# Attention core with its maxima as a row of the contraction, two buffers of queries and keys, scores three steps behind the looks

## The chip, the cores and the metric

One core of a Trainium2 chip runs the whole program. The metric is device microseconds of one execution. TensorE does matrix products, VectorE and ScalarE work on its results, GpSimd helps and issues transfers, SyncE only issues transfers (DMAs).

## The reference

Input x is 4 images of 16x16 positions with 192 channels, float32. Four blocks follow each other; each adds a mixer and a feed-forward part to x, each behind a layer norm. The mixers of blocks 0, 2 and 3 are attentions with 12 heads of 16 channels over the 256 positions of an image. This is blocks 2 and 3:

```python
attn = einsum('bqc,bkc->bqk', q * SCALE, k)
attn = attn + rel_h[..., :, None] + rel_w[..., None, :]   # rel_h, rel_w: q times tables of relative position
attn = softmax(attn, axis=-1)
out = einsum('bqk,bkc->bqc', attn, v)
```

Block 0 is a local attention: every position sees 9 neighbours at distance 1, 2 or 3 (by head), positions outside the image count as zeros. Block 1's mixer is a Fourier mixer, and the feed-forward parts are mixtures of experts; the change leaves their arithmetic alone.

## The kernel before

`attention(net, m, prep)` is called for l0, l2 and l3 (attention 0, 2, 3). First TensorE projects x to queries, relative terms, keys and values (`project_tensor`, `project_scalar`, `project_vector`). Queries and keys are split into a high and a low part, so that one product with reduced precision over stacked parts gives the full one; `store` writes the parts to `q_scratch` and `k_scratch` in DRAM, and `load_queries` and `load_keys` bring them back with 128 stacked rows in the one pair of buffers `q_parts`, `k_parts`. The load of a new image's piece (4, 2, 4, 2 heads) waits until the scores of the same heads of the image before are done. One-hot rows in the keys (from `onehot_scratch`) and, in l0, rows of 0 or a huge negative number in the queries (`near_scratch`) add the positional terms and the mask.

The core goes by pairs of heads: 6 pairs an image, 4 images, 24 steps (n). All engines run the same list of steps, each its own part, in an order written out by hand; the first image (on GpSimd the first two) is unrolled, the rest is a loop over images:

- `look` (TensorE, L803): queries times keys, positions of the query on the partitions, two banks of PSUM for the two heads.
- `maximum` (VectorE, L917): one reduction over the pair gives the negated row maxima; in l0 L921 lets the padding in.
- `shift` (L990 GpSimd, L926 VectorE): identity times maxima, a diagonal matrix per head and half.
- `score` (TensorE, L815 and L816): keys times queries, transposed against the look, and on top a product of ones with the shift, which subtracts each query's maximum. It comes 2 steps after the look in l0, 1 step after in l2 and l3.
- `exponential` (ScalarE, L877) writes the probabilities; `mix_quad` (TensorE, L854) multiplies them with v for four heads; `take_mix` (ScalarE, L883) copies, `turn` (TensorE, L823) transposes back, `finish` (VectorE, L942 to L954) divides by the row sum.

In the core SyncE loads the next images (`load_image`) and stores a part of the images 2 and 3, GpSimd stores the rest of them piece by piece between shifts (`store_rest`), stages v (`stage_v`, L981) and in l0 stores the finished heads. Tables for later blocks (`prep.third`) go out from SyncE in groups of four in l0. `attention_output` then projects the result; in l0 it first rereads it from DRAM (L1041).

## Time and profile before

| | us |
|---|---|
| median of 3 runs | 777.36 |
| runs | 773.33 to 778.35 |
| the profiled execution (its span) | 779.2 |
| first look to last finish, attention 0 | 37.4 to 109.4 |
| attention 2 | 391.1 to 455.7 |

The profiled execution's own time beside its span is not listed separately; the span, from the first to the last instruction, is used for it. Times of rows count from the start of the span. Engines in the rows: PE is TensorE's matmul, PEld its weight load, DVE is VectorE, ACT ScalarE, POOL GpSimd, SP SyncE; a name with q is the engine's queue. A group's "idle before" is time in which the engine did nothing, and the arrow names what ended it. The granted clock of TensorE is a share of full speed (2.4 GHz); 0.50 is the lower of its two levels.

### The profile page before, as it was taken

To read this page: it belongs to the slowest core of one execution; us is meant where nothing else is said; L and a number is where in the kernel's file an instruction comes from. 1 tells how busy PE (TensorE), PEld (TensorE's weight loads), DVE (VectorE), ACT (ScalarE), POOL (GpSimd) and SP (SyncE) were. 2 spreads that over 40 slices of the span, in tenths; PEclk is the share of its full clock that TensorE was granted. 3 is DMA by queue.
4 is the path that set the end of the run, shared out by engine and by line. 5 is a ranking of instruction groups with operands and counts; after the bars stand their busy time and mean duration, and the time that the engine had idled before them with its cause. 6 is when DMAs were issued, how large, how long until landed. Compare 5 with 4: busy or idle time off the path is not lost. (4 is left out here: it accounts for less than half of the span.)

```text
span 779.2 us, 14121 instructions
## 1 busy us (share of the span) xinstructions
PE 707.0 (91%) x4658; PEld 612.0 (79%) x4658; DVE 392.7 (50%) x983; ACT 301.7 (39%) x604; POOL 227.0 (29%) x271
## 2 busy tenths in 40 slices
PE   4987988999998999998888988899999896999997
PEld 2566767897796899995676778699999666777996
DVE  4466746015345443335678756334435476875301
ACT  3334533332413344424444552233452253555323
POOL 4166620002100044442055301723344204531000
PEclk9989999899999999999979999989999998999999
DMA  3735540534106166533788403567772279850352
GB/s 92 197 107 150 143 115 22 142 102 121 30 1 179 45 167 167 127 48 71 207 203 217 102 17 117 156 156 167 185 174 28 55 188 236 227 121 1 101 135 70
DMA packets 94011, 95.22 MB, mean 122 GB/s; under 512 B 18881, under 2 KB 80213, under 8 KB 93945
## 3 DMA queue, kind: packets, MB, share of 16 engines
q1 hardware_dynamic: 80568, 75.11, 36.6%
q0 software_dynamic: 11712, 18.18, 11.4%
q10 hardware_dynamic: 1680, 1.28, 0.6%
q8 instruction: 29, 0.48, 0.3%
q14 instruction: 22, 0.17, 0.1%
HBM read 66.92 MB, written 27.84 MB: 122 GB/s over the span
## 5 line engine op out<-in xcount | busy, mean ns | idle before, releaser
L2130 POOL DMA_INDIRECT sum_scratch<-area,f_row_index x48 | 72.4, 1509 | 172.3 <-DVE area L2053 157.0
L917 DVE TENSOR_REDUCE neg_max<-psum 128x4 f32<-128x1024 f32 x72 | 88.0, 1222 | 32.9 <-PE psum L803 32.0
L1804 PE MATMUL psum<-w,area 128*112 128x192 f32 (+1 forms) x576 | 96.2, 326 | 0.0
L1804 PEld LDWEIGHTS psum<-w,area 128*112 128x112 f32 (+1 forms) x576 | 93.5, 183 | 0.0
L990 POOL TENSOR_TENSOR shift<-ident,neg_max 128x256 fp32r<-128x256 f32 x96 | 66.5, 704 | 89.1 <-DVE neg_max L917 57.4
L295 PE MATMUL psum<-ident 128*128 128x128 f32 x624 | 82.0, 289 | 5.1 <-issue 1.9
L295 PEld LDWEIGHTS psum<-ident 128*128 128x128 f32 x624 | 77.9, 204 | 7.2 <-issue 5.9
L815 PE MATMUL psum<-q_parts,k_parts 128*128 128x256 f32 x288 | 79.6, 306 | 0.3
L803 PE MATMUL psum<-k_parts,q_parts 128*128 128x256 f32 x288 | 56.0, 321 | 25.9 <-DMA k_parts<-k_scratch 15.0
L816 PE MATMUL psum<-shift,ones_r 128*128 128x256 f32 x288 | 75.2, 292 | 0.0
L803 PEld LDWEIGHTS psum<-k_parts,q_parts 128*128 128x128 f32 x288 | 42.7, 208 | 38.6 <-issue 20.7
L1911 DVE TENSOR_TENSOR q_parts<-w,q_parts 128x1536 fp32r<-128x1536 f32 x16 | 28.1, 1756 | 81.4 <-ACT q_parts L1841 81.4
L815 PEld LDWEIGHTS psum<-q_parts,k_parts 128*128 128x128 f32 x288 | 57.9, 201 | 10.4 <-issue 8.2
L877 ACT ACTIVATE area<-psum 128x512 f32<-128x512 f32 x96 | 52.4, 595 | 30.2 <-PE psum L816 30.1
L816 PEld LDWEIGHTS psum<-shift,ones_r 128*128 128x128 f32 x288 | 57.9, 201 | 0.0
L587 PE MATMUL psum<-x_wide,l_w 96*96 96x512 f32 x96 | 44.7, 622 | 3.5 <-PEq L158 2.8
L1869 ACT ACTIVATE area<-psum,b 128x384 f32<-128x384 f32 x48 | 27.9, 582 | 49.5 <-PE psum L1790 46.6
L1387 PE MATMUL psum<-x_wide,w 96*128 96x256 f32 x192 | 42.8, 381 | 1.0 <-DMA b<-in_f_b_dram 0.9
L1468 DVE TENSOR_TENSOR mixed<-psum,b 128x384 f32<-128x384 f32 x8 | 4.5, 558 | 77.7 <-PE psum L1399 77.7
L1387 PEld LDWEIGHTS psum<-x_wide,w 96*128 96x128 f32 x192 | 36.0, 190 | 6.6 <-DMA b<-in_f_b_dram 1.7
L854 PE MATMUL psum<-area,v_stage 128*32 128x256 f32 x384 | 39.4, 386 | 0.0
L587 PEld LDWEIGHTS psum<-x_wide,l_w 96*96 96x96 f32 x96 | 16.1, 171 | 28.9 <-issue 28.9
(258 smaller groups left out, 1329.9 us busy)
## 6 DMA issues: line engine op xcount, KB each, us to landing
w<-in_f_w_dram SPq DMA_DIRECT2D x32, 576.0 KB, 5.0
w<-in_f_w_dram SPq DMA_DIRECT2D x16, 384.0 KB, 4.7
w<-in_f_w_dram SPq DMA_DIRECT2D x32, 192.0 KB, 5.0
q_parts<-q_scratch SPq DMA_DIRECT2D x32, 192.0 KB, 3.5
q_scratch<-area SPq DMA_DIRECT2D x22, 192.0 KB, 2.2
k_parts<-k_scratch SPq DMA_DIRECT2D x63, 64.0 KB, 3.1
q_parts<-q_scratch SPq DMA_DIRECT2D x32, 96.0 KB, 2.9
q_parts<-q_scratch SPq DMA_DIRECT2D x40, 64.0 KB, 3.2
```

The source lines that it names most:

```text
L295: pe.matmul(net.psum[:, bank, 0:P], net.ident[:, :], net.ident[:, :], start=True, stop=True)
L587: ins = pe.matmul(ps[0:HC, bank, :], m.w[:, k, D * j + HC * half:D * j + HC * (half + 1)], net.x_chan[:, k, 512 * tc:512 * (tc + 1)], star ...
L803: ins = pe.matmul(ps[:, b, IMG_TOK * c:IMG_TOK * (c + 1)], query(2 * s + b, c), k_parts[:, 2 * s + b, :], start=True, stop=True)
L815: pe.matmul(out, k_parts[:, h, keys], query(h), start=True, stop=False)
L816: ins = pe.matmul(out, net.ones_r[:, :], net.shift[:, s % 2, b, :, :], start=False, stop=True)
L854: ins = pe.matmul(ps[32 * (h % 4):32 * (h % 4 + 1), 6, 0:IMG_TOK], net.v_stage[:, k, h, :], net.probs_t[h // 2 % 3][:, h % 2, k, :], start ...
L877: act.activation(net.probs_t[s % 3][:, b, :, :].rearrange("p k t -> p (k t)"), ps[:, 2 + 2 * (s % 2) + b, :], ACT.Exp).then_inc(exp_done, 1)
L917: ins = dve.tensor_reduce(most, ps[:, 0:2, :].rearrange("p b (c k) -> p (b c) k", c=2), AX_X, ALU.max, negate=True)
L990: ins = nc.gpsimd.tensor_tensor(*shift_of(n, s, b))
L1387: ins = pe.matmul(ps[:, 3 * b + fc // 2, IMG_TOK * (fc % 2):IMG_TOK * (fc % 2 + 1)], net.w1[0:HC, b, k, P * fc:P * (fc + 1)], net.x_chan[: ...
L1804: ins = pe.matmul(out, x.hidden[:, fc, R * c:R * (c + 1)], net.w2[:, b, fc, :], start=(fc == 0), stop=(fc == FCH - 1))
L2130: pool.indirect_dma_start(net.sum_dram[:, :], bass.IndirectOffsetOnAxis(ap=row_index[0:size, b, c:c + 1], axis=0), x.y[0:size, b, c, :], N ...
```

## The change

What it does:

- The negated maximum of each query becomes one more row of the contraction in the score (row `MAX_ROW` of `q_parts`, ones in the same row of `k_parts`). `maximum` now works head by head; `turn_maximum` (TensorE) transposes the pair's maxima [128, 4] to [4, 128] in PSUM, `take_row` (ScalarE) copies them to `max_rows`, and `set_row` (SyncE) writes them into the row with a DMA of 2 KB. Shifts and their matmuls go, with them `ones` and the memsets of `q_parts` at the start.
- `q_parts` and `k_parts` have a second buffer each (`Second`); images alternate. Loads go by halves of 6 heads. Image 0's come from SyncE and GpSimd, all others from GpSimd (`load_half`). The constant rows are loaded for both buffers in l0 and l2, for one in l3.
- `store_rest` stores the images 2 and 3 together, in 4 (l0) or 10 (l2, l3) DMAs, all from GpSimd behind the loads of image 1, and GpSimd waits for their landing before the loads of image 2 and before v of image 1 is staged.
- Looks are by head and alternate with the scores of three steps before (`BEHIND = 3`). The order of a step on TensorE: look head 0 of pair n, score head 0 of n-3, turn of the maxima of n-1, look head 1, score head 1, then the mix of a quad in odd steps and its turn in even ones. All steps are unrolled.
- The tables of the Fourier mixer are loaded in `attention_output` of l0, before the reread; the other tables go out one behind each `set_row`. `experts` takes a tile of its own (`marks`) in place of `shift`.

```diff
+BEHIND = 3
...
+    MAX_ROW = K0 + HD if m.local else K0 + QROWS
...
+            def set_row(n):
+                i, s = divmod(n, PAIRS_OF_HEADS)
+                sp.wait_ge(max_row_sb, n + 1)
+                dst = q_parts[i % 2][MAX_ROW:MAX_ROW + 1, 2 * s:2 * s + 2, :].bitcast(F32)
+                sp.dma_start(dst.rearrange("p n (c t) -> p (n c) t", c=2), net.max_rows[:, s % 3, :].bitcast(F32)).then_inc(row_set[s % 3], DMA)
...
+            for n in range(ALL_PAIRS):
+                set_row(n)
+                if prep:
+                    start_loads(net, sp, itertools.islice(tables, 1), prep.loaded)
...
-            def look(i, s):
-                need(pe, max_ready, n)
-                for b in range(2):
-                    for c in range(2):
-                        ins = pe.matmul(ps[:, b, IMG_TOK * c:IMG_TOK * (c + 1)], query(2 * s + b, c),
+            def look(n, b):
+                need(pe, max_ready, 2 * n + b - 1)
+                for c in range(2):
+                    ins = pe.matmul(ps[:, b, IMG_TOK * c:IMG_TOK * (c + 1)], q_parts[buf][0:MAX_ROW, h, P * c:P * (c + 1)],
+                                    k_parts[buf][0:MAX_ROW, h, :], start=True, stop=True)
...
+            def turn_maximum(n):
+                if m.local:
+                    pe.wait_ge(max_known, n + 1)
+                else:
+                    pe.wait_ge(max_ready, 2 * n + 2)
+                need(pe, max_row_sb, n)
+                pe.transpose(ps[0:4, 7, 0:P],
+                             net.neg_max[:, 2 * s:2 * s + 2, :].rearrange("p n c -> p (n c)"), net.ident[:, :]).then_inc(max_turned, 1)
...
-                        pe.matmul(out, k_parts[:, h, keys], query(h), start=True, stop=False)
-                        ins = pe.matmul(out, net.ones_r[:, :], net.shift[:, s % 2, b, :, :], start=False, stop=True)
+            def score(n, b):
+                need(pe, exp_done, 2 * (n - 2) + b + 1)
+                if b == 0:
+                    pe.wait_ge(row_set[s % 3], DMA * (2 * i + s // 3 + 1))
+                for k in range(2):
+                    ins = pe.matmul(ps[:, 2 + 2 * (s % 2) + b, IMG_TOK * k:IMG_TOK * (k + 1)],
+                                    k_parts[buf][0:MAX_ROW + 1, h, P * k:P * (k + 1)], q_parts[buf][0:MAX_ROW + 1, h, :],
+                                    start=True, stop=True)
...
+            for n in steps:
+                if is_pair(n - BEHIND):
+                    exponential(n - BEHIND, 0)
+                if is_pair(n - 1):
+                    take_row(n - 1)
+                if is_pair(n - BEHIND):
+                    exponential(n - BEHIND, 1)
+                if quad_of(n, 2) is not None:
+                    take_mix(quad_of(n, 2))
...
+            def load_half(i, half):
+                need(pool, scored, (i - 2) * HEADS + HALF_HEADS * (half + 1))
+                load_queries(pool, i, half, loaded[i % 2][half])
+                load_keys(pool, i, half, loaded[i % 2][half])
...
+            pool.wait_ge(first_loaded[0], per_load)
+            for half in range(2):
+                load_half(1, half)
...
+            store_rest(pool)
+            pool.wait_ge(rest_written, DMA * rest_count)
+            for i in range(IMGS - 1):
+                if i + 2 < IMGS:
+                    load_half(i + 2, 0)
+                stage_v(i + 1, 0)
...
+            fourier_loads = fourier.loads(dram)
+            prep.third += fourier_loads
+            attention_output(net, l0, norm, [(gate.loads, gate.loaded), (fourier_loads, prep.loaded)], gate.mean)
```

## Rows read from the trace of the kernel before

**Rows 1.** By line, maxima: attention 0, 2, 3, stretches of 0, 2 (ns min/median/max)

```profile
L917 DVE TENSOR_REDUCE neg_max<-psum x24: 1208/1225/1226, 39.4 to 100.5; 128x4 f32<-128x1024 f32 x24
L917 DVE TENSOR_REDUCE neg_max<-psum x24: 1211/1224/1225, 392.3 to 449.1; 128x4 f32<-128x1024 f32 x24
L917 DVE TENSOR_REDUCE neg_max<-psum x24: 1212/1224/1226, 650.0 to 705.1; 128x4 f32<-128x1024 f32 x24
L917 DVE TENSOR_REDUCE neg_max<-psum x6: 1225/1225/1225, 88.4 to 100.5; 128x4 f32<-128x1024 f32 x6
L917 DVE TENSOR_REDUCE neg_max<-psum x7: 1215/1225/1225, 435.0 to 449.1; 128x4 f32<-128x1024 f32 x7
```

**Rows 2.** Attention 2, busy by stretch (counts), granted clock, DMA share, GB/s

```profile
391.00:398.70 7.70, 6.32 (x28) 6.06 (x28) 5.31 (x8) 1.95 (x4) 3.58 (x6) 0.50 0.92 214
398.70:455.70 57.00, 52.45 (x478) 41.58 (x477) 42.93 (x79) 29.14 (x58) 27.05 (x44) 1.00 0.57 144
```

**Rows 3.** Timeline, attention 0: start, length, engine, line, operation

```profile
49.95 1.09 PE L854 MATMUL psum<-area,v_stage 128*32 128x256 f32 x16
...
77.15 0.38 PE L823 MATMUL psum<-ident,mix_chan 128*128 128x128 f32 x2
77.67 0.74 PE L803 MATMUL psum<-k_parts,q_parts 128*128 128x256 f32 x4
78.45 1.22 DVE L917 TENSOR_REDUCE neg_max<-psum 128x4 f32<-128x1024 f32 x1 [0.43 <-PE psum L803]
79.09 0.28 PE L816 MATMUL psum<-shift,ones_r 128*128 128x256 f32 x1
79.88 0.17 DVE L942 TENSOR_TENSOR pad_exp<-pad_exp,pad_count 128x8 f32<-128x8 f32 x1
80.55 0.37 ACT L883 COPY mix_chan<-psum 128x256 f32<-128x256 f32 x1 [0.16 <-PE psum L854]
80.62 0.36 DVE L954 TENSOR_TENSOR mixed<-psum,inv_sum 128x64 f32 x2
```

**Rows 4.** Timeline of attention 0, the look that begins image 2

```profile
71.50 1.22 PE L803 MATMUL psum<-k_parts,q_parts 128*128 128x256 f32 x4 [3.81 <-DMA k_parts<-k_scratch]
```

**Rows 5.** Costliest groups of the page: the exponentials

```profile
L877 ACT ACTIVATE area<-psum 128x512 f32<-128x512 f32 x96 | 52.4, 595 | 30.2 <-PE psum L816 30.1
```

**Rows 6.** DMA: attention 2 in sum; median us to landing, quiet, full queues

```profile
DMA packets 10136, 9.83 MB, mean 154 GB/s; under 512 B 1867, under 2 KB 9492, under 8 KB 10132
...
f_slot_number<-in_f_slot_number_dram SPq DMA_DIRECT2D x1, 1.5 KB, 1.8
...
k_parts<-k_scratch ACTq DMA_DIRECT2D x3, 32.0 KB, 5.0
```

**Rows 7.** Looks grouped, attention 0, 2, 3; timeline of ends of 0, 2

```profile
L803 PE MATMUL psum<-k_parts,q_parts x96: 278/283/575, 37.4 to 100.2; 128*128 128x256 f32 x96
L803 PE MATMUL psum<-k_parts,q_parts x96: 274/283/582, 391.1 to 448.8; 128*128 128x256 f32 x96
L803 PE MATMUL psum<-k_parts,q_parts x96: 278/283/582, 648.8 to 704.8; 128*128 128x256 f32 x96
...
109.02 0.36 DVE L954 TENSOR_TENSOR mixed<-psum,inv_sum 128x64 f32<-128x64 f32 x2
...
451.16 0.39 PE L815 MATMUL psum<-q_parts,k_parts 128*128 128x256 f32 x1
455.36 0.36 DVE L954 TENSOR_TENSOR mixed<-psum,inv_sum 128x64 f32<-128x64 f32 x2
```

**Rows 8.** Timeline of the output stage of attention 0

```profile
111.24 0.39 SPq L1041 DMA_DIRECT2D mixed<-o_scratch  x1
116.54 1.04 PE L1068 MATMUL psum<-ident,mixed 128*96 128x128 f32 x8
```

**Rows 9.** Timeline of the start, and landing of the input

```profile
3.58 2.65 POOL L289 MEMSET q_parts<- 64x3072 f32 x1
...
x_res<-in_x_dram ACTq DMA_DIRECT2D x1, 384.0 KB, 4.5
```

More of the change, by code:

```diff
@@ L646, in project_scalar @@
         for b in range(4):
-            if b == 2:
-                act.wait_ge(first_written[of_keys], 2 * DMA)
-                for piece in range(2):
-                    load_keys(act, 0, piece)
             act.wait_ge(k_sb, b + 1)
@@ L758, in _ @@
+            tables = iter(prep.third if prep else ())
             for n in range(of_keys + 1):
                 store_first(n)
+            for n in range(0, of_keys, 2):
+                written(n)
+            load_queries(sp, 0, 0, first_loaded[0])
+            store_first(of_keys + 1)
             for half in range(2):
-                for n in range(half, of_keys, 2):
-                    written(n)
-                for piece in (2 * half, 2 * half + 1):
-                    load_queries(sp, 0, piece)
@@ L856, in mix_quad, with turn @@
                 ins.then_inc(mixed_ps, 1)
-            project_tensor(pe)
-            for _ in all_steps(pe, step):
-                pass
-            last = IMGS * PAIRS
-            if behind == 2:
-                score(last - 2, PAIRS - 2)
-            mix_quad(IMGS - 1, GROUPS - 2)
-            score(last - 1, PAIRS - 1)
-            turn(IMGS * GROUPS - 2)
-            mix_quad(IMGS - 1, GROUPS - 1)
-            turn(IMGS * GROUPS - 1)
+            def turn(quad):
+                pe.wait_ge(mix_sb, quad + 1)
+                for c in range(2):
+                    ins = pe.transpose(ps[:, 6, IMG_TOK + P * c:IMG_TOK + P * (c + 1)], net.mix_chan[:, P * c:P * (c + 1)], net.ident[:, :])
+                ins.then_inc(turned, 1)
@@ L955, in finish @@
                 ins.then_inc(mixed_sb, 1)
[L957 to L973 removed]
+            project_vector(dve)
+            for n in steps:
+                for b in range(2 if is_pair(n) else 0):
+                    maximum(n, b)
+                if m.local and is_pair(n):
+                    allow_padding(n)
+                if quad_of(n, 3) is not None:
+                    finish(quad_of(n, 3))
         @block.gpsimd
@@ L1019, in _ @@
+            for n in range(1, of_keys, 2):
+                pool.wait_ge(first_written[n], 2 * DMA)
+            load_queries(pool, 0, 1, loaded[0][1])
             pool.wait_ge(v_sb, 1)
@@ L1520, in __init__ @@
         self.low = net.sb("tokens_low", [P, TILES, D], F32R)
[L1521 to L1522 removed]
+        self.is_slot = [spare[:, TILES * D:TILES * D + SLOTS_MAX], *(net.marks[:, n, :] for n in range(2))]
         free = rest
```

416 lines of the change are left out of this document (174 added, 242 removed).

## The prediction

> **What bounds the kernel now.** I looked first at what attention costs and what holds its step. Each of the three attentions runs 24 head pairs. Grouped by line, the row maxima start at 39.4 and end at 100.5 us in attention 0, at 392.3 to 449.1 in attention 2, at 650.0 to 705.1 in attention 3; undisturbed stretches give 12.1/5 = 2.43 us a step in attention 0 and 14.1/6 = 2.35 in attention 2 [rows 1]. By stretch, TensorE is busy 52.5 of 57 us at a granted clock of 1.00, but 0.50 in the first 7.7 us [rows 2]: a core stage starts at half clock. In the timeline of two steps at full clock [rows 3] the eight score matmuls end with one at 79.09, 1.42 us after the look began at 77.67, twelve matmuls in all, so one costs 0.12 us. A mix of a quad takes 1.09 us [rows 3]; its turn, two transposes, 0.24 at the same pace (0.38 busy with the drain). Two steps are thus 24 x 0.12 + 1.1 + 0.24 = 4.2 us of TensorE against 4.7 measured; the rest is waiting for the maximum. So TensorE bounds attention 2 and 3 to about 90%; in attention 0 VectorE is close behind, and a load comes late once: the look at 71.50 waited 3.8 us for keys [rows 4].
>
> **The change, part by part.** All by hand from durations at full clock.
>
> *Shift matmuls out.* Per pair four of twelve matmuls go (96 per attention, 0.12 us apart) [rows 3]: -0.48 us. Added is one transpose of the maxima, no row has its shape; between 0.12 (half of a turn's 0.24) and 0.38 (its busy time with the drain) [rows 3]; I take 0.13, since the drain is not waited for by TensorE. Two steps: 16 x 0.12 + 0.26 + 1.1 + 0.24 = 3.5, with waits 3.75: 1.87 us a step.
>
> *Maximum by head.* A reduction of 1,024 elements takes 1.22 us [rows 1]. One of 512 has no row: from 0.61 (half) to 0.78 (half with a further 0.17, what the smallest VectorE operation here costs [rows 3]); I take 0.69. Four in two steps: 2.76. The finish of a quad in attention 0 runs from 79.88 to 80.98, 1.1 us [rows 3]; with the padding operations, 0.6 per two steps, and gaps that makes 4.7 us, 2.35 a step: VectorE bounds attention 0 (2.2 to 2.5), so little of the matmul saving shows there. In attention 2 and 3 the finish has no padding, 0.6 us: 3.5 in two steps, below TensorE's 3.75. The two heads' banks alternate, so the next look no longer waits for the whole pair. GpSimd's 1.2 us of shifts a pair goes, off the path.
>
> *The row's way.* Score of pair m comes three steps after its look; its maxima are turned one step after. From the end of score (m-2, head 0), all on one chain: drain 0.3, an exponential that stands ahead on ScalarE 0.6 [rows 5], the copy of the row 0.25 (between 0.17, above, and the 0.37 of a copy of 128x256 [rows 3]), semaphores and SyncE 0.1, then the DMA, L. It must fit in two steps less one score: step >= 0.75 + L/2. The smallest loads land after 1.8 us in an idle stretch; a 32 KB one took 5.0 us with the queues full [rows 6]. This row is 2 KB, on a queue that holds nothing else in attention 2 and 3: nearest to the first. I take 2.0 quiet and 2.7 while bulk runs, so 1.75 hidden under 1.87, and 2.1 exposed. In attention 0 (2.35) up to L = 3.2 is hidden. But SyncE also issues one weight table behind each row there; two of these are 432 KB, some 2 us of transfer in front of the next row: +2.
>
> The Trainium skill ("DMA: Bandwidth & Descriptors", section "Queues, rings and completion order") says that a DMA engine goes round its queues packet by packet. By that rule bulk on GpSimd's queue would delay a row hardly at all; the 5.0 us row speaks against, though that transfer stood behind three of its own queue. The rule makes a rival below.
>
> *Fill and tail.* From the first look to the first score, three steps of looks alone: half-clock look and two reductions 2.4, turn and copy 0.8, SyncE 0.1, L 2.7: 6. In attention 0 VectorE is still with the values at that time: 7. The tail: look 23 to score 23 is 4.7 (reduction 1.0, turn, copy, L); score 23 to the last finish is as before, 451.16 to 455.7 = 4.6, and 5.0 in attention 0, ending at 109.4 [rows 7].
>
> *Half clock.* TensorE is idle in the fill, so it starts the dense part at the low level; I give it 4 us there, in which one step passes instead of two.
>
> *Loads and buffers.* The second buffer lets image i+1 load during image i: the 3.8 us wait goes, with the half-clock steps behind it; 23 x (2.66 - 2.43) = 5.3 us in attention 0 [rows 1, 4]. The price: GpSimd now issues all of it in one queue, image 1 (by the code 12 DMAs of 160 rows of 12 KB, 1.97 MB in attention 2 and 3), then the stores of images 2 and 3 in one piece (10 DMAs, 3.1 MB), waits for their landing, and only then loads image 2; behind that wait stands the staging of v for image 1, for which TensorE's mix of quad 3 waits in step 11. 9.83 MB moved in 64 us at a mean share of 0.61 [rows 2, 6], so 250 GB/s at full. 0.3 + 1.97 + 3.1 = 5.4 MB are 21.5 us, and image 2's first half another 4: 26 to 29 us after the start with landings. Step 12 is due at 6 + 4 + 17 = 27: +1 in attention 2 and 3. In attention 0 only 3.3 MB stand ahead, 13 us, due at 30: none. Also, half 0 and half 1 of image 0's queries now load side by side, and the first look needs six heads in place of four: +1 at the start of attention 2 and 3, nothing in attention 0, whose queries are a third.
>
> The skill's same page (section "SWDGE vs HWDGE vs iDMA") warns that VectorE can hold up GpSimd's writing of descriptors. It would lengthen this queue; GpSimd's issues beside busy VectorE show no sign here, and it is part of the rival on bulk below.
>
> *Sums by attention.* Attention 2: 6 + 4 + 5.7 steps x 2.1 (bulk running, 12) + 13.3 x 1.9 (25.3) + 1 (later bulk) + 1 (image 2) + 4.7 + 4.6 = 58.6, after +1 at the start: 59.6 for 64.7 (391.1 to 455.7 [rows 7]): -5. Attention 3 is 63.0 now (648.8 to 705.1, and 6.6 from the last maximum to the end as in attention 2 [rows 1, 7]): +1 as well, -3.4. Attention 0: 7 + 4 + 19 x 2.35 + 4.7 + 5.0 + 2 (tables) = 67.4 for 72.0 (37.4 to 109.4): -4.6.
>
> *Beside the core.* The nine Fourier tables (1.2 MB) move from attention 0 to its output stage, on SyncE's queue ahead of the reread of image 3. That reread is issued at 111.24 and used at 116.54 [rows 8]; an issue takes 0.39 and a gap [rows 8], nine some 3.8, which puts it at 115, and 1.2 MB stand before it, 4.9 us: lands at 118.5, +2. Its bounds are 0 (projection hides all) and 4. The two memsets at the start end at 6.23, the input has landed at 0.89 + 4.5 = 5.4, and the barrier is at 6.5 [rows 9]: -0.6. Unrolling the image loop changes no count; no idle time by instruction fetch shows at the loop's ends, so 0.
>
> Sum: -5 - 3.4 - 4.6 + 2 - 0.6 = -11.6 us. The profiled execution spans 779.2, 1.8 above the median 777.36, so 777.4 - 11.6 = **766 us**.
>
> **Rivals.** *More: the steps run at TensorE's own pace* (by the round-robin rule of the skill cited above this is what follows). L stays at 2.0 under bulk, no wait for image 2, first look not later, a reduction of 0.62. Then attention 2 is 6 + 4 + 19 x 1.87 + 9.3 = 54.8 (-9.9), attention 3 -8.1, attention 0 at 2.2 a step -9.5; with -0.6: 749 to 750. For it: every term taken away is an allowance, none is in a row. Against: queues at 0.92 share early in the core [rows 2].
>
> *Slower: the row's DMA is the bound.* If L is 3.5 on average, a step is 0.75 + 1.75 = 2.5 in all three. The point is L = 3.2: there the step equals the 2.35 of now. Attention 2: 6.8 + 4 + 47.5 + 5.7 + 4.6 + 1 = 69.6 (+4.9), attention 3 +6.6, attention 0 7.8 + 4 + 47.5 + 5.7 + 5.0 + 2 = 72.0 (0), +2 and -0.6: 790. For: a wait on three other engines and a queue now lies in each step, and the 32 KB transfer landed after 5.0 us [rows 6]. Against: it is 16 times larger and had others of its own queue ahead.
>
> *No change: bulk or clock eats it.* Image 2 comes 5 us later in attention 2 and 3 (200 GB/s in place of 250 gives this), or gaps in TensorE's stream keep the clock at the low level for 4 us more per attention, each costing about 2 to 3: 774 to 778.
>
> **How the numbers follow.** Forecast 0.45, faster still 0.17, slower 0.16, no change 0.22. Within 1% of 777.4 (769.6 to 785.1) is what a measurement here can't tell from no change. The forecast's own spread, 758 to 774, puts a sixth of it within 1%: faster 0.38 + 0.17 + 0.01 = 0.56, same 0.07 + 0.20 = 0.27, slower 0.17. The range goes from 750 to 787, leaving out the far parts of the outer cases; the likeliest case's own is 758 to 774.
>
> **What would show it.** Starts of the single-head maxima: 1.9 us a step in attention 2 and 3, 2.35 in attention 0; waits of the score line on the row's DMA short in the later half, some tenths in the first; landing of the row's DMA 2.0 to 2.7; first score 6 us after the first look; the granted clock at 1.00 within 10 us of the start; reread of image 3 waited for by 2 us. It is wrong if the score line waits for the DMA in most steps, if quad 3's mix waits long for v, or if the clock stays low in the core.

## The result and the profile after

The changed kernel takes 811.94 us, median of 5 runs (803.99 to 814.47), against 777.36 for the kernel before (now also 5 runs, 773.33 to 779.12): a ratio of 1.044, interval 1.041 to 1.048. That is slower by 34.6 us where 11.6 less was forecast, and outside the range of 750 to 787. The two traces show only 23.0 of the 34.6 us (spans 802.2 and 779.2): the profiled run of the changed kernel is the fastest of its five, 8.0 us below the median, and with the same 1.8 us between time and span (803.99 for 802.2) the profiled run of the kernel before is an estimated 3.6 us above its own. Among all runs below only two of the ten of e16_direct_order_2_half, its profiled one with them, are over 1.5% above the fastest of their kernel and count as slow; its ratio leaves them out, and the median of the other eight is 771.0.

The head maxima by line, in attention 0, 2 and 3 and in a stretch of attention 2, answer to [rows 1]:

```profile
L905 DVE TENSOR_REDUCE neg_max<-psum x48: 680/687/692, 41.1 to 103.0; 128x2 f32<-128x512 f32 x48
L905 DVE TENSOR_REDUCE neg_max<-psum x48: 680/691/693, 399.0 to 462.8; 128x2 f32<-128x512 f32 x48
L905 DVE TENSOR_REDUCE neg_max<-psum x48: 680/691/693, 662.9 to 725.0; 128x2 f32<-128x512 f32 x48
...
L905 DVE TENSOR_REDUCE neg_max<-psum x9: 680/680/692, 455.5 to 462.8; 128x2 f32<-128x512 f32 x9
```

One takes 0.69 us, as estimated. In the last stretch eight intervals, four steps, take 7.3 us: 1.83 us a step, which is the forecast's 1.87. But the maxima of attention 2 run from 399.0 to 462.8, 63.8 us where the kernel before needed 56.8 [rows 1]. The good steps are there, but they lie at the end, where no bulk (the loads and stores of whole images) is in flight.

Windows of attention 2, beside [rows 2]: the whole core stage, then pieces of 4 us. The columns are the length, the busy time of PE, PEld, DVE, ACT and POOL (instructions in brackets), the granted clock, the DMA share and GB/s.

```profile
398.20:471.10 72.90, 56.06 (x432) 41.59 (x432) 37.20 (x84) 35.84 (x85) 27.53 (x52) 0.81 0.55 130
...
402.00:406.00 4.00, 1.59 (x6) 1.00 (x5) 2.03 (x3) 1.54 (x2) 4.00 (x8) 0.50 1.06 201
406.00:410.00 4.00, 2.26 (x9) 1.93 (x9) 1.38 (x2) 1.33 (x3) 4.00 (x8) 0.50 1.07 193
410.00:414.00 4.00, 2.44 (x10) 2.10 (x11) 1.38 (x2) 1.33 (x3) 0.99 (x2) 0.50 1.00 356
414.00:418.00 4.00, 4.00 (x25) 2.48 (x26) 0.69 (x1) 1.67 (x4) 0.00 (x0) 0.50 1.03 415
418.00:422.00 4.00, 4.00 (x37) 3.24 (x35) 3.05 (x7) 2.59 (x7) 2.40 (x5) 0.82 0.38 120
422.00:426.00 4.00, 1.90 (x14) 1.57 (x13) 2.45 (x6) 1.59 (x4) 3.49 (x8) 1.00 1.05 185
...
458.00:462.00 4.00, 4.00 (x42) 3.25 (x41) 3.29 (x10) 3.16 (x8) 0.35 (x1) 1.00 0.02 5
```

The same window of the core stage in the kernel before:

```profile
391.10:455.70 64.60, 58.73 (x504) 47.57 (x504) 48.13 (x86) 30.99 (x61) 30.63 (x50) 0.94 0.61 152
```

Read three things there. Where the DMA share is 1.0, TensorE is busy for 1.6 to 2.4 of 4 us in four of the five pieces (in the fifth, 414 to 418, it works all the time, but at half clock); where the share is 0.02, it is busy all of the time and at full clock. The clock stands at 0.50 for the first 20 us, in which TensorE is idle for a good part of each 4 us until 414, and its mean in the core falls from 0.94 to 0.81. And 72 matmuls fewer leave the busy time at 56.1 for 58.7, since more of them run at the low level, while the idle time goes from 5.9 to 16.8 us: what was saved in matmuls is given back by the clock, and the idle time comes on top.

What TensorE waits for is in its timeline at the first scores (start, length, line; in brackets the idle time and what ended it), with SyncE's issues of rows behind it:

```profile
398.22 0.98 PE L796 MATMUL psum<-k_parts,q_parts 112*128 112x256 f32 x3 [8.04 <-DMA k_parts<-k_scratch]
406.59 0.77 PE L817 MATMUL psum<-q_parts,k_parts 113*128 113x256 f32 x2 [1.93 <-DMA q_parts<-max_rows]
410.52 0.80 PE L817 MATMUL psum<-q_parts,k_parts 113*128 113x256 f32 x2 [1.67 <-DMA q_parts<-max_rows]
413.85 0.76 PE L817 MATMUL psum<-q_parts,k_parts 113*128 113x256 f32 x2 [1.04 <-DMA q_parts<-max_rows]
...
401.10 19.05 SPq L761 DMA_DIRECT2D q_parts<-max_rows  x6
```

The row of pair 0 is issued at 401.10 and its score starts at 406.59: 5.5 us, issue included, for 2 KB. Steps there take 3.3 to 3.9 us. Over the whole execution, from the costliest groups of the page:

```profile
L817 PE MATMUL psum<-q_parts,k_parts 113*128 113x256 f32 (+1 forms) x144 | 37.5, 350 | 20.4 <-DMA q_parts<-max_rows 20.4
L817 PE MATMUL psum<-l_q_parts_second,l_k_parts_second 113*128 113x256 f32 (+1 forms) x144 | 30.5, 304 | 13.2 <-DMA l_q_parts_second<-max_rows 13.2
```

33.6 us of waits for rows, in all three attentions (9.4, 13.2 and 11.0), but not in each step: there are 26 of them in 72 steps (7, 10 and 9). The looks and the output stage of attention 0 answer to [rows 7, 8]: from the projection's start to the first look 25.7, 35.2 and 34.7 us in attention 0, 2, 3, for 22.2, 30.9 and 31.0; reread of image 3 issued at 117.44, its transposes at 120.92 with no idle time before them.

### The profile page after: what moved, and what is told of

It is laid out like the page before. It is cut to its first block and busy times, and to the rows that moved or that the text cites. A ratio compares the mean times of both kernels' runs of the same rounds, so it can differ in the third digit from the quotient of the medians.

```text
span 802.2 us, 12853 instructions
## 1 busy us (share of the span) xinstructions
PE 697.3 (87%) x4442; PEld 593.4 (74%) x4442; DVE 371.4 (46%) x1005; ACT 315.5 (39%) x676; POOL 212.6 (27%) x265
## 5 line engine op out<-in xcount | busy, mean ns | idle before, releaser
L905 DVE TENSOR_REDUCE neg_max<-psum 128x2 f32<-128x512 f32 x144 | 95.9, 687 | 89.1 <-PE psum L796 88.7
L796 PE MATMUL psum<-k_parts,q_parts 112*128 112x256 f32 (+1 forms) x144 | 43.8, 404 | 22.9 <-DMA k_parts<-k_scratch 21.5
L817 PE MATMUL psum<-q_parts,k_parts 113*128 113x256 f32 (+1 forms) x144 | 37.5, 350 | 20.4 <-DMA q_parts<-max_rows 20.4
L796 PEld LDWEIGHTS psum<-k_parts,q_parts 112*128 112x128 f32 (+1 forms) x144 | 29.9, 260 | 31.5 <-issue 22.7
L830 PE MATMUL psum<-area,v_stage 128*32 128x256 f32 x384 | 45.4, 459 | 3.2 <-DVE mixed L941 3.0
L817 PEld LDWEIGHTS psum<-q_parts,k_parts 113*128 113x128 f32 (+1 forms) x144 | 28.9, 246 | 24.1 <-issue 17.8
L817 PE MATMUL psum<-l_q_parts_second,l_k_parts_second 113*128 113x256 f32 (+1 forms) x144 | 30.5, 304 | 13.2 <-DMA l_q_parts_second<-max_rows 13.2
L796 PE MATMUL psum<-l_k_parts_second,l_q_parts_second 112*128 112x256 f32 (+1 forms) x144 | 39.3, 358 | 0.0
L868 ACT ACTIVATE x_wide<-psum 128x512 f32<-128x512 f32 x48 | 28.1, 592 | 26.9 <-PE psum L817 26.6
L1853 ACT ACTIVATE area<-psum 128x320 f32<-128x320 f32 x48 | 21.0, 438 | 42.6 <-PE psum L1774 42.6
```

What stands on the lines that cost most here:

```text
L796: ins = pe.matmul(ps[:, b, IMG_TOK * c:IMG_TOK * (c + 1)], q_parts[buf][0:MAX_ROW, h, P * c:P * (c + 1)], k_parts[buf][0:MAX_ROW, h, :], s ...
L817: ins = pe.matmul(ps[:, 2 + 2 * (s % 2) + b, IMG_TOK * k:IMG_TOK * (k + 1)], k_parts[buf][0:MAX_ROW + 1, h, P * k:P * (k + 1)], q_parts[bu ...
L830: ins = pe.matmul(ps[32 * (h % 4):32 * (h % 4 + 1), 6, 0:IMG_TOK], net.v_stage[:, k, h, :], net.probs_t[h // 2 % 3][:, h % 2, k, :], start ...
L868: act.activation(net.probs_t[s % 3][:, b, :, :].rearrange("p k t -> p (k t)"), ps[:, 2 + 2 * (s % 2) + b, :], ACT.Exp).then_inc(exp_done, 1)
L905: dve.tensor_reduce(net.neg_max[:, h, :], ps[:, b, :].rearrange("p (c k) -> p c k", c=2), AX_X, ALU.max, negate=True).then_inc(max_ready, 1)
L1853: act.activation(x.hidden[:, fc, 0:used], ps[:, 2 + (2 * b + fc) % HIDDEN_BANKS, 0:used], ACT.Relu, bias=net.b1[:, b, fc:fc + 1] if with_b ...
```

## The experiments

Theory A: the row's DMA takes 4 to 6 us while bulk is in flight, and the scores wait for it. Rivals: the order or lateness of the images (B), the queue it is on (C), the delayed first look (D). The letters in the expectations are those of each run. Each run has its own median of the kernel before, taken on the same chip (773.9 to 775.7). Of attention 2 each run's windows gave:

```
                          us     ratio  95% interval    to 1st look  core   rows  images  clock
before                  777.36                              30.9     64.6     -    2.0    0.94
changed kernel          811.94   1.044  1.041 - 1.048       35.2     72.7   13.2   1.1    0.81
e1_no_wait              780.92   1.005  1.001 - 1.008       35.3     66.8    -     5.9    0.84
e2_no_bulk              767.31   0.988  0.983 - 0.993       35.2     55.7    3.8   0      0.87
e3_half_later           813.49   1.050  1.045 - 1.055       31.6     77.6   17.9   3.5    0.82
e4_behind5              792.19   1.020  1.016 - 1.025       35.1     64.4    1.9   5.2    0.81
e5_swap                 822.71   1.061  1.053 - 1.069       34.9     76.4   15.6   0      0.77
e6_direct               782.96   1.009  1.005 - 1.013       34.4     64.7    -     7.7    0.86
e7_by_image             807.14   1.043  1.037 - 1.049       34.9     74.7   14.5   1.4    0.81
e8_direct_swap          783.65   1.013  1.010 - 1.016       34.4     66.5    -    10.0    0.87
e9_layout               812.10   1.048  1.042 - 1.053       35.6     76.0   15.4   0      0.77
e10_direct_layout       781.90   1.008  1.005 - 1.011       34.6     63.9    -     6.8    0.86
e11_direct_all          785.13   1.014  1.010 - 1.019       31.4     72.0    -    12.2    0.83
e12_before_layout       775.30   1.000  0.997 - 1.002
e13_order               803.55   1.037  1.031 - 1.043       35.6     72.6   15.4   0      0.83
e14_direct_order        782.95   1.013  1.005 - 1.022       34.6     65.6    -     5.9    0.85
e15_direct_order_2      776.33   1.002  0.998 - 1.005       35.2     62.2    -     3.0    0.88
e16_direct_order_2_half 773.00   0.995  0.991 - 0.999       31.9     63.4    -     3.4    0.87
e17_two_queues          772.33   0.996  0.993 - 1.000       34.7     59.1    -     2.6    0.93
e18_two_queues_half     770.40   0.993  0.990 - 0.996       31.1     62.3    -     3.7    0.88
```

"To 1st look" is from the projection's first matmul to the first look, "core" from there to the end of the last finish, "rows" and "images" TensorE's waits for a row's DMA and for queries, keys or staged v behind the first look, in us. In e11, e16 and e18 "images" includes one wait (2.3, 1.7 and 2.8 us) of the look of pair 3 that the profile puts down to "issue". It is the wait for the second half of image 0's queries: in e18 their last DMA, issued at 389.96, takes 6.8 us to land, and the look starts at 396.85.

### Taking the wait or the bulk away

**e1_no_wait.** The row's DMAs go to a spare place and the row stays zero, so the maxima are not subtracted.

```
-                dst = q_parts[i % 2][MAX_ROW:MAX_ROW + 1, 2 * s:2 * s + 2, :].bitcast(F32)
+                dst = net.marks[8 + s % 3:9 + s % 3].rearrange("p a b -> p (a b)")[:, 0:2 * IMG_TOK].bitcast(F32)
...
-                if b == 0:
-                    pe.wait_ge(row_set[s % 3], DMA * (2 * i + s // 3 + 1))
```

> Everything stays, the turn, the copy and the 2 KB DMA of each row too, but the DMA writes to a spare place, the row of the contraction holds zeros, and no score waits for it (left out: the subtraction of the maxima). Theory A, the landing of the row's DMA while GpSimd's bulk runs is what holds the steps: the waits on it (33.6 us in the profiled execution, of them some 9 in attention 0) go and TensorE reaches its high level earlier: 25 to 40 us less than the changed kernel, 772 to 787. Theory B, the bulk itself (data of images 2 and 3 late, v staged late) and the later first look hold it: the waits only move, 5 to 10 less.

780.92: 31 us less than the changed kernel, inside A's 25 to 40, with every DMA still issued. The DMA costs by being waited for, as A has it. Its waits of TensorE, though, show what had been hidden behind it (line waited for: total, times, longest):

```profile
PE psum L809 <- ACT max_rows L876: 4.7, 3, 2.5
PE psum L798 <- DMA k_parts<-k_scratch: 3.6, 1, 3.6
PE psum L830 <- POOL v_stage L961: 2.3, 1, 2.3
```

The first is this run's own (ScalarE waits for an old row's DMA before it writes the buffer again); the other two are image 2's keys and image 1's v, late now that the steps are fast.

**e2_no_bulk.** The stores and loads of images 2 and 3 are left out, so these are computed from the data of images 0 and 1; rows are sent and waited for as in the changed kernel. This kernel leaves work out, so its time is not one that the full program could reach; it serves to read the steps.

```
-            store_rest(pool)
-            pool.wait_ge(rest_written, DMA * rest_count)
...
-                if i + 2 < IMGS:
+                if False:
```

> The stores of images 2 and 3 and their loads are left out (these images then use the queries and keys of images 0 and 1), the row path stays whole. Theory A: without bulk the row's DMA takes about 2 us, hidden under steps of 1.9; the core of attention 2 goes from 72.7 us to about 58, that of attention 3 likewise, attention 0 by 5 less: 30 to 38 us less in all. Theory C, the row's way is too long even in quiet: steps stay at 2.4 or more, 10 to 15 us less. The expert parts may differ by a few us since their input differs, so the core stages decide.

767.31: 45 us less, more than the 30 to 38 expected. Row waits fall from 33.6 to 10.2 us, and what is left of them (3.8 in attention 2) lies at the first steps, while image 1 loads (3.6 of it before 404). Its windows:

```profile
395.00:399.00 4.00, 1.72 (x7) 1.14 (x6) 2.03 (x3) 1.54 (x2) 3.26 (x6) 0.50 1.07 195
...
407.00:411.00 4.00, 4.00 (x45) 3.05 (x38) 2.96 (x7) 2.86 (x8) 0.00 (x0) 1.00 0.00 1
```

In 411.3 to 436.6 us 29 maxima, 14 steps, are 1.81 us apart. With the DMA engines quiet the forecast's arithmetic of a step holds: the row is back in time in every one. So the row's time depends on what else is in flight, and both runs together leave A and, behind it, B.

**e3_half_later.** The second half of image 0's queries is issued behind the first half's keys.

```
-            load_queries(pool, 0, 1, loaded[0][1])
             pool.wait_ge(v_sb, 1)
...
             pool.wait_ge(first_loaded[0], per_load)
+            load_queries(pool, 0, 1, loaded[0][1])
```

> Only the order of GpSimd's list changes: the queries of image 0's second half are loaded after the keys of the first half have landed, no longer beside them. If side by side is what makes the first look of attention 2 and 3 4.3 us later than before, it comes 2 to 4 us earlier in both: 4 to 8 us less in all, unless the later second half makes step 3 wait. If the first half's own bytes are the limit: no change.

813.49, no gain. The first look does come at 31.6 and 31.4 us after the projection's start in attention 2 and 3 in place of 35.2 and 34.7, so D names the cause of that delay rightly; but the half is then late for pair 3 and rows wait 17.9 us for 13.2. What was won at the start was lost again in waits further on.

**e4_behind5.** Scores five steps behind the looks in attention 2 and 3 (six row buffers), three in attention 0.

```
+    BEHIND = 3 if m.local else 5
-                    pe.wait_ge(row_set[s % 3], DMA * (2 * i + s // 3 + 1))
+                    pe.wait_ge(row_set[s], DMA * (i + 1))
```

> Scores five steps behind in attention 2 and 3 (six places for rows and six semaphores in place of three; attention 0 stays at three). The row's DMA then may take four steps less 1.5 us: some 6 us at 1.9 a step. Theory A: the 24 us of waits in attention 2 and 3 shrink to a few, 10 to 20 us less. Theory B: the looks run further ahead, wait for the same data, no change, or slower by the longer tail (2 to 4 us).

792.19: 20 us less. Row waits in attention 2 and 3 go from 24.2 to 3.8 us, so two more steps hide nearly all of the row's landing; waits for image 2 go from 2.1 to 12.7 (5.2 and 7.5). Attention 0, which kept three, keeps its 9 us of waits. The clock still stands at 0.50 for 18 us in attention 2 (401.1 to 419.1), with only 1.9 us of row waits, so these are not all that holds it.

### Queue, size of pieces, order of the bulk

**e5_swap.** SyncE issues the images' loads and stores, GpSimd the rows.

```
-                sp.dma_start(dst.rearrange("p n (c t) -> p (n c) t", c=2), ...
+                pool.dma_start(dst.rearrange("p n (c t) -> p (n c) t", c=2), ...
...
-                load_queries(pool, i, half, loaded[i % 2][half])
+                load_queries(sp, i, half, loaded[i % 2][half])
```

> Queues swapped: SyncE issues the loads of images 1 to 3 and the stores of images 2 and 3, GpSimd issues the row of each pair (and image 0's second half of queries, as before). Theory A (a row waits behind what is in flight on the DMA engines, whoever issued it): rows still land 4 to 6 us after their issue while bulk runs, the score line waits about as long as in the changed kernel (33.6 us in all); only the rate may help: in the kernel before, SyncE's queue moved 248 to 257 GB/s at a full share (384 to 392 us), GpSimd's in the changed one 156 to 185 in its image loads, so bulk ends some 15 us earlier in attention 2 and 3 and about a third of the waits go: 790 to 803. Theory B (it is GpSimd's queue, with some 3 KB a packet against 1 KB on SyncE's, that holds up the small transfer): the waits on rows fall to under 10 us and images come sooner: 765 to 782. Theory C (the queue of the row is what matters, and GpSimd's takes longer to start a transfer than SyncE's): slower than the changed kernel, over 812.

822.71, slower still; row waits are 48.4 us (13.5, 15.6, 19.3). The time lies in the range given to C (over 812) and outside A's 790 to 803, so by the time alone C would have won; the landings decide. On GpSimd's queue the DMA view gives the landings (issues, KB each, median us to landing), in 407 to 424 us, where the DMA share is over 1.0, and in 456 to 478, where it is 0.06:

```profile
q_parts<-max_rows POOLq DMA_DIRECT2D x5, 2.0 KB, 5.4
...
l_q_parts_second<-max_rows POOLq DMA_DIRECT2D x6, 2.0 KB, 1.6
```

The same 2 KB by the same queue: 5.4 us (3.5 to 5.9) and 1.6. That is L itself, the landing time of the row's DMA in the forecast's sum. It goes by what is in flight, and the queue hardly counts: from issue to first score 5.5 us pass here (407.98 to 413.51) as they do in the changed kernel, and GpSimd adds about 0.3 us, since its issue starts 0.29 us after ScalarE's copy of a row has ended (415.05 to 415.34) and SyncE's 0.02 (412.09 to 412.11). Nor does SyncE's queue move bulk faster here: 178 to 182 GB/s at a share of 1.09 to 1.14 in the first 8 us of image 1's load, so the gain that A's range counted on was not there. What makes this kernel 11 us slower than the changed one is not taken apart; GpSimd's list, where the rows now stand behind the staging of v, is edited too.

The Trainium skill ("DMA: Bandwidth & Descriptors", section "Issuing engines are not separate DMA queues") says that all queues end on the same 16 DMA engines and that another issuer saves only issue time. This run agrees: the row lands after 5.4 us on a queue that has no bulk. The rule of the Trainium skill that an engine goes round its queues by packets (same page, "Queues, rings and completion order"), from which the forecast took a rival, is not borne out as a promise of a short wait: 5.4 us for 2 KB on a queue without bulk of its own.

**e6_direct.** No DMA for the row: four matmuls with one column of weights each put the maxima of a pair on one partition of PSUM, and ScalarE copies them into row 0 of the queries (loads land one partition lower down, and zeros are loaded into row 0 with each image). Everything is computed.

```
-                pe.transpose(ps[0:4, 7, 0:P], ...
+                for j in range(4):
+                    ins = pe.matmul(ps[0:1, 7, P * j:P * (j + 1)], net.neg_max[:, 2 * s + j // 2, j % 2:j % 2 + 1],
+                                    ident_r, start=True, stop=True)
...
+                act.copy(q_parts[...][0:1, 2 * s:2 * s + 2, :].rearrange("p n t -> p (n t)"), ps[0:1, 7, :])
```

> No DMA for the maxima: they are turned onto one partition by four matmuls with one column of weights each and copied by ScalarE straight into row 0 of the queries (data one partition lower down, zeros loaded into row 0 with each image); bulk, queues and order as in the changed kernel; the full computation. If the row's DMA is the whole loss, this gives what the run with no wait on rows gave, 781, plus ScalarE's longer copy (one partition x 512, some 0.6 us as the exponential of 512, for 0.24: 0.36 a step, 72 steps; ScalarE was busy about 3.2 of 4 us at 1.87 us a step, so steps come to about 2.0 and 0.15 x 72 = 11 of it shows) and TensorE's three more matmuls (0.06 to 0.12 us each): 781 to 797. If most of the loss were late image loads rather than rows, it stays over 800.

782.96: 29 us less than the changed kernel, and 2 us above the run that waits for no row (ratios 1.009 and 1.005). The copies and the maxima while bulk runs, by line:

```profile
L868 ACT CAST q_parts<-psum x5: 557/558/574, 399.0 to 407.1; 1x512 fp32r<-1x512 f32 x5
...
L899 DVE TENSOR_REDUCE neg_max<-psum x15: 681/691/692, 403.2 to 416.7; 128x2 fp32r<-128x512 f32 x15
```

14 intervals, seven steps, in 13.5 us: 1.93 us a step at a DMA share of 1.0 for most of the stretch (0.72 in its last 2 us), where the changed kernel takes 3.3 to 3.9 at its half clock. Later, at a share of 0.01, 15 intervals of the same maxima (436.2 to 450.5) make 1.91 a step. So A is settled from the other side: the same work with a way on chip hardly notices the bulk. Image waits are 7.7 and 6.7 us in attention 2 and 3.

**e7_by_image.** Stores of image 2 ahead of its load, those of image 3 behind.

```
+            store_rest(pool, 2)
...
+                if i == 0:
+                    store_rest(pool, 3)
```

> The stores split by image: image 2's ahead, its load behind them, then image 3's stores, then image 3's load; bytes the same, number of store DMAs twice (10 to 20 in attention 2 and 3, 0.56 to 0.7 us of GpSimd each). Theory A: the rows wait as long as DMA engines are full, and that is as long as before in sum: within 1% of the changed kernel, 804 to 820. The rival from the forecast, that it is the late load of image 2 (its wait for the whole of the stores) that costs: 1.55 MB at 410 GB/s is 3.8 us earlier for image 2 in attention 2 and 3: 800 to 806.

807.14: 5 us less, intervals overlapping with the changed kernel's. With rows still waited for, order hardly matters.

**e8_direct_swap.** Direct rows, and all bulk on SyncE.

> Both: maxima copied into place by ScalarE with no DMA, and all bulk issued by SyncE. Steps no longer wait for rows, and image loads move at SyncE's rate (about 250 GB/s for 170): 2 MB an image in 8 us, under the 12 us of six steps, so image 2 and 3 are in time. From the run without bulk (767) plus ScalarE's longer copies (up to 11): 762 to 778. If SyncE's queue is no faster in this place, as the run with the direct row alone.

783.65, no better than e6_direct: the expectation that SyncE's queue is faster was wrong. TensorE's timeline at step 12 shows where it goes:

```profile
416.25 1.09 PE L855 MATMUL psum<-area,v_stage 128*32 128x256 f32 x16
427.30 0.80 PE L819 MATMUL psum<-k_parts,q_parts 113*128 113x256 f32 x2 [9.96 <-DMA k_parts<-k_scratch]
```

Without row waits image 2 is 10 us late, and the clock falls again behind it (0.50 in 424 to 428).

**e9_layout, e10_direct_layout, e12_before_layout.** The DRAM copies with the image outermost, so that a row of a load is one piece of 6 KB (4 and 2 KB in the last); e9 on the changed kernel, e10 on e6_direct, e12 on the kernel before.

```
-        self.q_dram = nc.dram_tensor("q_scratch", [2, 2, 3, HC, IMGS, IMG_TOK], F32, kind="Internal").ap()
+        self.q_dram = nc.dram_tensor("q_scratch", [2, 2, IMGS, 3, HC, IMG_TOK], F32, kind="Internal").ap()
```

> The changed kernel, with the image outermost in the DRAM copies of queries and keys, so that the six heads of one row of a load are 6 KB in one piece in place of six pieces of 1 KB, 4 KB apart (the stores of images 2 and 3 write 1 KB pieces in place of 2 KB, 14 DMAs in place of 10). The image loads moved 156 to 185 GB/s at a full share, the stores 405 to 415. Theory A (a row waits for as long as bulk fills the DMA engines, and bulk takes long because of its small pieces): at the stores' rate an image is in after 5 us in place of 11.6, six to seven loads of 1.97 MB take some 35 us less DMA time, row waits fall to a third, image 2 comes in time: 772 to 785. Rival (the time of a load goes by its bytes or by GpSimd's writing of descriptors, not by piece): nothing moves, 806 to 818.

> Row without a DMA, and the image outermost in DRAM. Of the run with the direct row (783) what was left was the wait for image 2: 7.3 + 2.8 us for keys and 4.9 for the staged v in attention 2, with half-clock steps behind. If loads take 5 us an image that goes: the steps of 1.98 us run through, core of some 24 x 1.98 + 5.3 + 3.5 + 2 = 58 us for 64.5 in attention 2 and 3: -13, and up to 2 each from an earlier first look: 766 to 772. If loads are no faster: 780 to 785.

> The kernel before the change, with the image outermost in DRAM and nothing else: pieces of 1 KB become 4 or 2 KB (heads 4 and 2 to a piece). Its waits for keys (3.8 us at 71.50 in attention 0, some in attention 2 and 3) and its full queues ahead of the first look shrink: 765 to 773. If loads are no faster: 772 to 780.

812.10, 781.90 and 775.30: no gain in time, three times. Over 8 us of image 1's load in attention 2 and 3, at a full share, e9 moves 169 and 173 GB/s (the changed kernel 193 and 194) and e10 195 and 189 (e6 173 twice), and stores stay near 400; none comes near the stores' rate, so the size of a piece in DRAM is not what makes loads slow. What does was not found; a load writes 16 or 48 partitions, a store reads 96, and no run changes that.

**e11_direct_all.** e10_direct_layout with e7's and e3's edits.

> As the one before, and also the stores by image (image 2's ahead) and the second half of image 0's queries issued behind the first half's keys. The late queries brought the first look forward from 35 to 31.5 us after the start of attention 2 and 3; with no row to wait for it should now be kept in part: 760 to 768. If the second half then comes late for step 3, it equals the run before.

785.13, a miss by 17 to 25 us. First look at 31.4, core 72.0: image waits 12.2. The stores of image 2, issued from 397.1, are waited for until 412.6, while the DMA share, full until 410.2, is 0.09 in the next 2 us: the DMA engines run dry while a landing is awaited.

**e13_order, e14_direct_order, e15_direct_order_2, e16_direct_order_2_half.** Stores of image 2 first, then image 1, the first half of image 2, stores of image 3, the second half: alone (e13), with the direct row (e14), with scores two steps behind (e15), and with e3's edit too (e16).

```
+            store_rest(pool, 2)
             for half in range(2):
                 load_half(1, half)
...
-BEHIND = 3
+BEHIND = 2
```

> The changed kernel, rows by DMA, with the bulk in another order: the stores of image 2 first, then the load of image 1, then (stores of image 2 landed by then) the first half of image 2, the stores of image 3, the second half. Theory A (rows wait as long as the DMA engines are full; the bytes are the same): no gain over the split by image (807), 800 to 810. Rival (the order of images was the loss): 785 to 795.

> Row copied in place by ScalarE, and the new order of the bulk. At 11.6 us an image and 3.8 us an image of stores, from the first look: stores of image 2 to 3.8, image 1 to 15.4, image 2's first half to 21.2, its second, behind image 3's stores, to 30.8; due by steps of 1.98 us at 23 and 29. So the 10 to 12 us of waits for image 2 in the run with the direct row (783) shrink to about 3: 8 us less in attention 2 and 3 each and nothing in attention 0: 765 to 770. If bytes, not order, bound it: 778 to 783.

> As e14_direct_order with scores two steps behind the looks in place of three, which the row without a DMA allows: a step less in fill and in tail, 2 to 3 us in each of three attentions, if nothing is late for it: 758 to 764. The images are due a step earlier against the scores, so part may be given back.

> As e15_direct_order_2, with image 0's second half of queries issued behind the first half's keys. It brings the first look 3 to 4 us forward in attention 2 and 3, as in the two runs that had it; both gave it back in the wait for the second half, or for image 1, and so does this one if the DMA engines are the bound from the first look on: within 3 us of the run before. If it is kept: 5 to 7 us less.

803.55, 782.95, 776.33, 773.00; e14 and e15 miss their 765 to 770 and 758 to 764 by 12 us or more. The order alone gives 8 us by the medians with rows by DMA, but the intervals of the two ratios overlap (1.031 to 1.043, 1.041 to 1.048), and none with direct rows: in e14 image 2 is late by 2.6 and 1.3 us in attention 2 and 3, where e6 had 7.7 and 6.7, but image 1 is now 3.3 and 3.4 us late behind the stores (GpSimd needs 5.8 us to issue them, 391.05 to 396.82 in e15). That was overlooked in the expectations. The step less gives 7 us, with intervals that just touch. e3's edit brings 3 more by the medians, with intervals that overlap a little; in its trace part of the earlier first look goes into the wait of 1.7 us for the second half.

**e17_two_queues, e18_two_queues_half.** e15 and e16 with the stores issued by SyncE, beside GpSimd's loads.

```
+            sp.wait_ge(first_loaded[0], per_load)
+            store_rest(sp, 2)
+            sp.wait_ge(loaded[1][1], per_load + DMA)
+            store_rest(sp, 3)
```

> As e15_direct_order_2 (776), with the stores of images 2 and 3 issued by SyncE (image 3's after image 1 has landed) beside GpSimd's loads of images. If GpSimd's issuing (0.53 to 0.57 us a DMA) made image 1 late, 3 us less in attention 2 and 3 each, with the half-clock steps behind: 766 to 771. If the DMA engines' rate did, it stays within 3 us of 776.

> As e16_direct_order_2_half (773), with the stores issued by SyncE. As above, and the wait for image 0's second half shrinks too, since it is issued first on a queue of its own: 761 to 768 by the one, 770 to 776 by the other.

772.33 and 770.40. e18 beats both kernels, by 0.7% of the one before (0.4 to 1.0). e17 is 4 us below e15 where 5 to 10 were expected, with intervals that overlap; e18 lies in the 770 to 776 that was given to the rate of the DMA engines. In e17 image 1 is late by 0.7 us in place of 3.0, so GpSimd's issuing was part of what delayed it, and the dense part holds, at a DMA share of 0.71 to 0.91:

```profile
400.00:404.00 4.00, 3.93 (x43) 3.04 (x40) 2.97 (x7) 3.38 (x7) 0.00 (x0) 1.00 0.80 246
404.00:408.00 4.00, 3.93 (x43) 3.01 (x42) 3.11 (x7) 3.23 (x8) 3.04 (x6) 1.00 0.71 166
408.00:412.00 4.00, 3.94 (x43) 3.02 (x42) 3.11 (x7) 3.37 (x7) 4.00 (x9) 1.00 0.91 255
412.00:416.00 4.00, 2.12 (x20) 1.85 (x18) 1.85 (x5) 1.91 (x4) 1.23 (x3) 1.00 1.09 330
```

Its core stages are 59.1, 58.2 and 61.1 us (attention 2, 3, 0), for 64.6, 62.9 and 72.0 before. The first look, still 3.6 to 4.2 us later than before, takes back 11.5 of these 21 us. In e18 the first look of attention 2 and 3 is back where it was, but the wait for image 0's second half (2.8 and 3.0 us) makes the cores 62.2 us each.

## Why the prediction was wrong

**The step that failed is "The row's way": L, the landing of the row's DMA, taken as 2.0 us quiet and 2.7 with bulk.** Quiet, it was even too long (1.6 in e5_swap; in e2_no_bulk steps of 1.81 us without waits). With bulk it is not 2.7 but 5.4 (e5_swap), and in the changed kernel row 0's score starts 5.5 us after the issue; by the forecast's own formula, step = 0.75 + L/2, 5.4 makes 3.45 us, and the steps there take 3.3 to 3.9 (at half clock, for which the formula has no term). I had the row that said so, 5.0 us for 32 KB with the queues full [rows 6], and put it aside because that transfer was larger and had others of its own queue ahead; e5_swap shows that the queue is not what counts. The trace of the kernel before also had a small transfer that I did not look at: 16 loads of 3.0 KB on SyncE's queue for the expert parts (`b` from `in_f_b_dram`) land after 5.3 us in the median, right behind loads of weights of up to 576 KB. The terms that came of it: the dense part of attention 2, first score to last look (406.6 to 462.0), took 55.4 us where the sum had 43.3; of attention 3 54.0; of attention 0 53.9 where it had 50.7. The tail was right (8.9 for 9.3).

**The rival "Slower: the row's DMA is the bound" was the right one**, 790 at L = 3.5, and had 0.16. It too was short, since it let the step grow but not the clock: I had the half clock end 10 us after the first look (6 of fill, 4 of dense part), and it stood for 20 in attention 2. The waiting steps thus cost twice, by the idle time and by the clock. That the row waits prolonged it is shown by e6_direct, which with the same bulk is at full clock 8 to 10 us after its first look. They are not all that held it: e4_behind5 has 1.9 us of row waits in attention 2 and stands at half clock for 18 us. One sign that I had named did not come: the score line waits in 26 of 72 steps, not in most.

**First look.** +1 was forecast in attention 2 and 3 and nothing in attention 0; measured are +4.3, +3.7 and +3.5. The six heads and the second half's loads were named, their size was not: e3_half_later brings 3.6 and 3.3 us back by one moved call. In the fill 8.4 us passed for 6 (attention 2), again L (5.5 for 2.7).

**Bulk and buffers.** 250 GB/s was read from a share of 0.61 over a mix [rows 2, 6]. In stretches of one kind loads move mostly 140 to 210 GB/s and stores 380 to 420: image 1 and the stores ahead of image 2 then need an estimated 1.97 MB / 0.175 + 3.1 / 0.41 = 18.8 us, no more than was forecast. What was mis-sized is image 2's load behind them. In e6_direct GpSimd waits 9.2 us for the stores' landing, until 23.1 us after the first look (394.2 to 417.3), and only then issues it; its keys land after 6.0 us, and image 2's first look comes at 426.3, so 9 us after the stores landed, where the forecast had 4 for this load. Image 2 was due there at about 417. In the changed kernel this shows only as 1.1 us in attention 2, behind the row waits; e1, e4, e6 and e8 uncover 5 to 10. The rival "No change" had priced it at 5 us in attention 2 and 3.

**What was right.** The step without waits (1.83 for 1.87), the reduction (0.69), the row's copy on ScalarE (0.24 for 0.25), and the start (-0.5 for -0.6). The term of 0.1 for semaphores and SyncE holds too (0.02 us from the copy's end to the issue); the issue itself, 0.57 us, is part of a landing time, which counts from its start.

**What was right by luck.** The output stage of attention 0 did get 1.8 us longer for the 2 forecast (second group of transposes 7.9 us after the first, for 6.2), but not by the reread behind the Fourier tables: the transposes at 120.92 follow the projection without a wait. The clock did it: from 112 to 121 it was 0.54 and then 0.50, where the kernel before had 1.00 for the first transposes and 0.64 for the projection, and the first eight transposes took 1.92 us for 1.05.

**The sum.** Against the forecast the trace shows: first looks +9.5 (11.5 measured, 2 forecast), cores +4.2, +14.1, +12.5 (attention 0, 2, 3), what lies around them -5.8: 34.5, which to rounding is the 34.6 between 23.0 measured and -11.6 forecast. Of the -5.8, -5.7 lie between attention 2 and 3, where the change edits nothing. They look like spread between executions: from the last finish of attention 2 to the projection of attention 3 the trace of the kernel before shows 162.0 us, the longest of all, e12_before_layout 154.4, and the others 155.2 to 160.7.

What stays open: why the other four timed runs are 6 to 10 us above the profiled one. e9_layout, whose profiled span is 811.4, has 39.8 us of row waits for 33.6, which fits but doesn't show it.

## What to carry to other kernels

Before a small DMA goes into each step of a loop, find what else is in flight during that loop: price its landing from a transfer in a stretch as busy as the loop's busiest, and don't count on its being small or alone on its queue (here 5.4 us for 1.6). If the loop can't be made deep enough, bring the data into place on chip (here 0.56 us of ScalarE and four short matmuls, for a DMA of 1.6 to 5.4 us). Where the bulk is the limit, price loads and stores apart, each from a stretch of its own, and count the issuer's time and the wait for landings; and price each new gap in TensorE's stream with the clock that it keeps low.

## What the runs showed of the hardware

- 2 KB from SBUF to SBUF landed in 1.6 us at a DMA share of 0.06 and in 5.4 at over 1.0 (medians, e5_swap), on GpSimd's queue beside bulk on SyncE's; on SyncE's queue beside bulk on GpSimd's 5.5 us passed from issue to use (changed kernel).
- At a full DMA share, loads of queries and keys from DRAM moved mostly 140 to 210 GB/s in stretches of 2 us, and stores of the same data 380 to 420; with pieces of 6 KB in DRAM for 1 KB the loads stayed below 200 over 8 us (169 to 195).
- A matmul with one column of weights over 128 columns (fp32r) took 0.22 us, and 128x1 weights loaded in 0.08. Four of them and a copy of one partition x 512 (0.56 us), in place of one transpose and a copy of four partitions x 128 (0.24 us), make a step of 1.91 us in a quiet stretch (e6_direct), for 1.81 to 1.83 (e2_no_bulk, changed kernel).
